# A post-norm transformer layer on one Trainium2 core: attention by chunks of 512 queries and four heads, with fp32r two-part scores and V projected last

## What is computed

```python
Q, K, V = X @ Wq + bq, X @ Wk + bk, X @ Wv + bv        # 2048 x 256, 16 heads of 16
scores = einsum('bhqd,bhkd->bhqk', q, k) / sqrt(16)
out = einsum('bhqk,bhkd->bhqd', softmax(scores), v)
out = out.transpose(0, 3, 2, 1).reshape(b, s, 256)     # (feature, head) by token, as one flat row order
x = layernorm(X + out @ Wo + bo)
gate, up = silu(x @ Wg * s_gate), x @ Wu * s_up        # int8 weights, 1024 wide
x = layernorm(x + (gate * up) @ Wd * s_down)
```

## Time and profile before

| | us |
|---|---|
| three runs | 695.58 (median), 695.06, 698.11 |
| span of the profiled execution | 694.9 |
| PE busy | 668.3 (96%) |
| ACT busy | 580.7 (84%) |
| DVE busy | 153.7 (22%) |
| POOL busy | 38.1 (5%) |
| first exponential starts | 53.86 |
| granted TensorE clock, mean | 0.991 |

### The profile page before, as it was taken

One profiled execution on the slowest core, in us unless ns is written; L12 is line 12 of the kernel. 1 busy time (PEld: TensorE's weight loads), 2 busy tenths in 40 slices (PEclk: granted clock), 3 DMA queues, 4 the chain that ended last, 5 costly groups with the idle time before them and its releaser, 6 DMA issues.

```text
span 694.9 us, 10890 instructions
## 1 busy us (share of the span) xinstructions
PE 668.3 (96%) x4002; PEld 259.4 (37%) x4002; DVE 153.7 (22%) x305; ACT 580.7 (84%) x657; POOL 38.1 (5%) x47
## 2 busy tenths in 40 slices
PE   8979999999999999999999999999999999999994
PEld 7852222222222222222222222222222257788884
DVE  6772000000000000000000000000000047756766
ACT  5748999999999999999999999999999943744442
POOL 3215000000000000000000000003000001000002
PEclk9998999999999999999999999999999999999998
DMA  8066132140404041321404040413000000000001
GB/s 233 19 71 69 13 35 31 17 46 3 46 0 46 0 46 12 34 29 17 45 1 46 0 46 0 46 12 34 0 0 0 0 0 1 1 0 32 0 30 60
DMA packets 15428, 19.50 MB, mean 28 GB/s; under 512 B 5912, under 2 KB 12336, under 8 KB 15408
## 3 DMA queue, kind: packets, MB, share of 16 engines
q1 hardware_dynamic: 14592, 18.97, 20.2%
q10 hardware_dynamic: 816, 0.26, 0.1%
HBM read 4.34 MB, written 2.10 MB: 9 GB/s over the span
## 4 chain that ended last, share of the span: by engine, by line
PE 89%; DVE 5%; issue 4%; ACT 1%; POOL 1%; DMA 1%; POOLq 0%; SPq 0%; DVEq 0%
PE ps L1061 37%; PE ps L1087 36%; PE ps L1184 7%; PE ps L1167 4%; PE ps L966 4%; DMA x_tok<-in_L_attn_X 1%; DVE at L769 1%; DVE stats L785 1%; DVE h L870 1%; PE ps L950 1%; DVE r_tmp L831 1%; ACT sg L549 0%; POOL rstd L431 0%; DVE x_tok L778 0%; PE ps L1155 0%
## 5 line engine op out<-in xcount | busy, mean ns | idle before, releaser
L510 ACT ACTIVATE probs<-ps 128x1024 f32<-128x1024 f32 x512 | 495.2, 1021 | 19.8 <-PE ps L1087 12.5
L1061 PE MATMUL ps<-probs,v_slot 128*32 128x512 f32 x2048 | 272.5, 605 | 4.7 <-issue 4.7
L1087 PE MATMUL ps<-q_stack,k_stack 100*128 100x512 bf16 x1024 | 267.6, 385 | 5.6 <-DVE k_stack L675 5.6
L1087 PEld LDWEIGHTS ps<-q_stack,k_stack 100*128 100x128 bf16 x1024 | 79.7, 98 | 280.8 <-ACT probs L510 213.1
L730 DVE TENSOR_SCALAR attn<-ps 128x512 f32 (+1 forms) x16 | 16.4, 1028 | 488.5 <-PE ps L1061 488.5
L1061 PEld LDWEIGHTS ps<-probs,v_slot 128*32 128x32 f32 x2048 | 40.9, 108 | 114.6 <-ACT probs L510 94.7
L549 ACT ACTIVATE sg<-ps,sgate_c 128x512 f32<-128x512 f32 x32 | 22.1, 690 | 46.7 <-PE ps L1184 46.5
L1167 PE MATMUL ps<-wd,h_hi 128*128 128x256 f32 x128 | 32.2, 285 | 2.3 <-DVE r_tmp L831 2.1
L1167 PE MATMUL ps<-wd,h_lo 128*128 128x256 f32 x128 | 31.9, 283 | 0.0
L870 DVE SCALAR_TENSOR_TENSOR h<-ps,sup_c,sg 128x512 f32<-128x512 f32 x32 | 24.0, 750 | 27.0 <-ACT sg L549 26.2
L1167 PEld LDWEIGHTS ps<-wd,h_hi 128*128 128x128 f32 x128 | 24.3, 190 | 4.9 <-DVE r_tmp L831 3.4
(11 more groups left out here) (100 smaller groups left out, 354.4 us busy)
## 6 DMA issues: line engine op xcount, KB each, us to landing
q_stack<-q_parts SPq DMA_DIRECT2D x16, 192.0 KB
k_stack<-k_parts SPq DMA_DIRECT2D x16, 192.0 KB
q_stack<-q_parts SPq DMA_DIRECT2D x16, 128.0 KB
k_stack<-k_parts SPq DMA_DIRECT2D x16, 128.0 KB
x_tok<-in_L_attn_X SPq DMA_DIRECT2D x3, 512.0 KB, 8.5
out<-out_tmp SPq DMA_DIRECT2D x3, 512.0 KB, 2.9
k_stack<-k_parts SPq DMA_DIRECT2D x16, 64.0 KB
q_stack<-q_parts SPq DMA_DIRECT2D x16, 64.0 KB
```

The costliest lines, as they stand in the source:

```text
L510: nc.scalar.activation(probs[:, (j * TT + kt) % 3, 2 * half:2 * half + 2, :].rearrange("p a b -> p (a b)"), ps[:, 2 * ring:2 * ring + 2, : ...
L1061: last = nc.tensor.matmul(ps[32 * q:32 * q + VW, ACC, :], v_slot[slot][:, kt, :], probs[:, n % 3, q, :], start=(kt == 0), stop=(kt == TT - 1))
L1087: last = nc.tensor.matmul(ps[:, 2 * ring + q % 2, :], k_stack[slot][0:ROWS, kt * P:(kt + 1) * P], q_stack[slot][0:ROWS, q * CW:(q + 1) * C ...
```

## The change

Attention is cut by chunks of 512 queries and quads of four heads: 16 steps (`STEPS`), each with all 2048 keys. A unit is one block of 128 keys for four heads of 512 queries, still two exponentials over 1024 columns. Q and K are kept as two fp32r parts; a head's stack has 51 rows (3 for bound and shift, 48 for three products), and the heads of a pair lie at rows 0 and 64 of the array. A slot (two of them) holds four heads, so that K is filled again for each chunk of queries. V is projected behind all of Q and K, DVE adds its bias straight from PSUM (`save_v`), POOL squares. At a step's end DVE copies bank 6 to `attn_q` (one of two), SP writes it to DRAM in another order (`move_out`, four DMAs) and, once per chunk, reads it back turned (`move_in`, two DMAs); DVE scales it in SBUF (`scale_attn`). The 64 transposes are gone. Loops of attention are written out instead of running in `Fori`. The DMA order on SP is: fill of slot s+2, shifts, at each fourth step move_in, then move_out of step s.

```diff
--- before.py
+++ after.py
-    PRODUCTS = [(3, 0, 0), (2, 1, 0), (1, 2, 0)]
-    SROW = sum(n for n, _, _ in PRODUCTS) * HD
-    MROW = SROW + 1
-    ROWS = MROW + 3
+    NQ = 4
+    QUADS = NH // NQ
+    STEPS = CH * QUADS
+    UPS = TT
+    UW = CW // HD
+    SHIFT_ROWS = 2
+    PROD = 1 + SHIFT_ROWS
+    ROWS = PROD + 3 * HD
+    HALF = 64
+    VW = HD + 1
...
+        k_parts = place("k_parts", [P, KO, 2, S], f32r, at)
...
+        k_slot = [place(f"k_slot{i}", [P, 2, S], f32r, at + 16 * KB * i) for i in range(NSLOT)]
...
+        q_slot = [place(f"q_slot{i}", [P, 2, CW], f32r, at + 4 * KB * i) for i in range(NSLOT)]
...
+        at32 = place("at32", [P, KO, VW, CH, UW], f32, at + 24 * KB)
+        attn_q = [place(f"attn_q{i}", [P, HD, UW], f32, at + 41 * KB + 2 * KB * i) for i in range(2)]
...
+        at_dram = nc.dram_tensor("at_dram", [CH, HD, NH, VW, UW], f32).ap()
...
-        V_AFTER = [(0, 1), (2, 3), (4,), (5, 6, 7)]
-        V_BANK = [4, 5, 4, 5, 4, 5, 4, 2]
+        V_BANK = [4, 5, 2, 3, 4, 5, 7, 6]
         NORM_BANK = [6, 7, 0, 1]
+        LAST_SQUARES = NQK - 4
...
+            def load_q(s, slot, hh, done):
+                h, base, c = NQ * (s % QUADS) + hh, HALF * (hh % 2) + PROD, s // QUADS
+                row, ko = HD * (h % HPB), h // HPB
+                dst, src = q_slot[slot].bitcast(f32), q_parts.bitcast(f32)
+                sp.dma_start(dst[base:base + 2 * HD, hh // 2, :],
+                             src[row:row + HD, ko, 0:1, c * CW:(c + 1) * CW].to_broadcast([HD, 2, CW])
+                sp.dma_start(dst[base + 2 * HD:base + 3 * HD, hh // 2, :],
+                             src[row:row + HD, ko, 1, c * CW:(c + 1) * CW]).then_inc(done, 16)
+            def load_k(s, slot, hh, done, first=0, last=S):
+                h, base = NQ * (s % QUADS) + hh, HALF * (hh % 2) + PROD
+                row, ko = HD * (h % HPB), h // HPB
+                dst, src = k_slot[slot].bitcast(f32), k_parts.bitcast(f32)
+                sp.dma_start(dst[base:base + 2 * HD, hh // 2, first:last],
+                             src[row:row + HD, ko, 0:2, first:last]).then_inc(done, 16)
+                sp.dma_start(dst[base + 2 * HD:base + 3 * HD, hh // 2, first:last],
+                             src[row:row + HD, ko, 0, first:last]).then_inc(done, 16)
+            def load_stack(s, slot, done):
+                for hh in range(NQ):
+                    load_k(s, slot, hh, done)
+                    load_q(s, slot, hh, done)
+            def load_shift(s, slot, done):
+                for hh in range(NQ):
+                    at, row = HALF * (hh % 2) + 1, NQ * s + hh
+                    sp.dma_start(q_slot[slot].bitcast(f32)[at:at + SHIFT_ROWS, hh // 2, :],
+                                 shift.bitcast(f32)[row:row + 1, :, :]).then_inc(done, 16)
+            def move_out(s):
+                c = s // QUADS
+                for hh in range(NQ):
+                    sp.dma_start(at_dram[c, :, NQ * (s % QUADS) + hh, :, :].rearrange("r d u -> d r u"),
+                                 attn_q[s % 2][32 * hh:32 * hh + VW, :, :]).then_inc(at_put[s % 2], 16)
+            def move_in(c):
+                for i in range(2):
+                    sp.wait_ge(at_put[i], 16 * NQ * (QUADS // 2) * (c + 1))
+                for ko in range(KO):
+                    sp.dma_start(at32[:, ko, :, c, :], at_dram[c, HPB * ko:HPB * (ko + 1), :, :, :]
+                                 .rearrange("r h d u -> (r h) d u")).then_inc(at_moved, 16)
+            sp.wait_ge(lo_ready, 1)
+            for hh in range(NQ):
+                load_q(0, 0, hh, stack_loaded[0])
+            sp.wait_ge(lo_ready, NQK - 6)
+            for hh in range(NQ):
+                load_k(0, 0, hh, stack_loaded[0], 0, S - CW)
+            sp.wait_ge(lo_ready, NQK - 2)
+            for hh in range(NQ):
+                load_k(0, 0, hh, stack_loaded[0], S - CW, S)
+            sp.wait_ge(lo_ready, NQK)
+            sp.wait_ge(v_psum, TT // 2)
+            load_stack(1, 1, stack_loaded[1])
...
+            load_shift(1, 1, stack_loaded[1])
+            for s in range(STEPS):
+                if s + NSLOT < STEPS:
+                    sp.wait_ge(scores_ready, 2 * UPS * (s + 1))
+                    load_stack(s + NSLOT, s % NSLOT, stack_loaded[s % NSLOT])
+                    load_shift(s + NSLOT, s % NSLOT, stack_loaded[s % NSLOT])
+                if s >= QUADS and s % QUADS == 0:
+                    move_in(s // QUADS - 1)
+                sp.wait_ge(attn_saved, s + 1)
+                move_out(s)
+            move_in(CH - 1)
...
+            act.wait_ge(v_psum, TT // 2)
+            for g in range(2 * UPS * STEPS):
+                u, p = g // 2, g % 2
+                ring = g % 3
+                act.wait_ge(scores_ready, g + 1)
+                if p == 0 and u >= 3:
+                    act.wait_ge(pv_done, u - 2)
+                nc.scalar.activation(
+                    probs[:, u % 3, 2 * p:2 * p + 2, :].rearrange("p a b -> p (a b)"),
+                    ps[:, 2 * ring:2 * ring + 2, :].rearrange("p a b -> p (a b)"),
+                    ACT.Exp, bias=0.0, scale=SCALE).then_inc(exp_done, 1)
...
+            def save_attn(s):
+                dve.wait_ge(pv_done, UPS * (s + 1))
+                if s >= 2:
+                    dve.wait_ge(at_put[s % 2], 16 * NQ * (s // 2))
+                nc.vector.tensor_copy(attn_q[s % 2][:], ps[:, ACC, :].rearrange("p (u r) -> p r u", r=HD)
+                                      ).then_inc(attn_saved, 1)
+            def scale_attn(c):
+                dve.wait_ge(at_moved, 16 * KO * (c + 1))
+                nc.vector.reciprocal(den[:], at32[:, :, HD, c, :]).then_inc(den_ready, 1)
+                dve.wait_ge(den_ready, c + 1)
+                nc.vector.tensor_tensor(at32[:, :, 0:HD, c, :], at32[:, :, 0:HD, c, :],
+                                        den[:].unsqueeze(2).to_broadcast([P, KO, HD, UW]), ALU.mult
+                                        ).then_inc(attn_scaled, 1)
+            for s in range(STEPS):
+                save_attn(s)
+                if s >= QUADS and s % QUADS == 1:
+                    scale_attn(s // QUADS - 1)
+            scale_attn(CH - 1)
...
+            def scores(g):
+                u, p = g // 2, g % 2
+                s, kt, ring = u // UPS, u % UPS, g % 3
+                slot = s % NSLOT
+                if kt == 0 and p == 0:
+                    pe.wait_ge(stack_loaded[slot], loaded(s))
+                    if s < NSLOT:
+                        pe.wait_ge(bound_ready, 2 * (s + 1))
+                    if s == 1:
+                        pe.wait_ge(late_ones, 2)
+                if g == 0:
+                    pe.wait_ge(norms_ready, 2)
+                elif g < 3:
+                    pe.wait_ge(v_ready, 2 * (g + 1))
+                else:
+                    pe.wait_ge(exp_done, g - 2)
+                for half in range(2):
+                    base = HALF * half
+                    last = nc.tensor.matmul(ps[:, 2 * ring + half, :],
+                                            k_slot[slot][base:base + ROWS, p, kt * P:(kt + 1) * P],
+                                            q_slot[slot][base:base + ROWS, p, :], start=True, stop=True)
+                last.then_inc(scores_ready, 1)
+            def prob_times_v(u):
+                s, kt = u // UPS, u % UPS
+                if u == 0:
+                    pe.wait_ge(v_ones, 1)
+                    pe.wait_ge(v_ready, TT // 2)
+                elif kt == 0:
+                    pe.wait_ge(attn_saved, s)
+                pe.wait_ge(exp_done, 2 * (u + 1))
+                for hh in range(NQ):
+                    last = nc.tensor.matmul(ps[32 * hh:32 * hh + VW, ACC, :],
+                                            v_all[:, kt, NQ * (s % QUADS) + hh, :],
+                                            probs[:, u % 3, hh, :], start=(kt == 0), stop=(kt == TT - 1))
+            UNITS = UPS * STEPS
+            for u in range(UNITS):
+                scores(2 * u)
+                scores(2 * u + 1)
+                if u >= 2:
+                    prob_times_v(u - 2)
+            prob_times_v(UNITS - 2)
+            prob_times_v(UNITS - 1)
...
+            pe.wait_ge(attn_scaled, CH)
```

More of the change, by code:

```diff
@@ L119, in layer_program @@
-        at = region(42 * KB)
-        w_raw = place("w_raw", [P, 3, KO * HID], f32, at)
-        w_hi = place("w_hi", [P, 3, KO, HID], f32r, at + 6 * KB)
-        w_lo = place("w_lo", [P, 3, KO, HID], f32r, at + 12 * KB)
-        rest = place("rest", [P, 4, CW], f32, at + 18 * KB)
-        squares = place("squares", [P, 4, S], bf16, at + 26 * KB)
-        attn = place("attn", [P, S // NH // 4, NH, NH], f32, at)
+        at = place_at[0]
+        v_all = place("v_all", [P, TT, NH, VW], f32)
+        w_raw = place("w_raw", [P, 3, KO * HID], f32, at)
@@ L143, in layer_program @@
-        yt_lo = place("yt_lo", [P, KO, S], f32r, at + 16 * KB)
+        squares = place("squares", [P, 4, S], bf16, at + 32 * KB)
```

(50 more changed lines are left out.)

456 lines of the change are left out of this document (149 added, 307 removed).

## The result

The changed kernel takes 709.15 us (median of four runs, 708.35 to 710.62) against 695.64 for the kernel before on the same chip: the ratio is 1.0193, 95% interval 1.0172 to 1.0214. It is slower by 1.9%. The forecast was 722 us, with 655 to 830 as its range. The profiled execution's span is 707.6 us where the forecast's sum came to 721.5.

What follows compares the result with a forecast made beforehand. SP's in-order DMA chain, 33.0 us a step against 29.4 of compute, was taken to bound attention. Last exponential at 571.4, plus 132.1 as before and 18 more behind attention, gave 721.5 of span, 722 us; range 655 to 830.

Steps and rivals of the forecast that it cites:

- The deciding term: Attention's DMA side: SP's in-order fill, shifts and one-engine writes take 33.0 us a step, more than 29.4 of compute.
- The price of a small packet: In move_out: a 128-byte packet costs 12.9 ns, between 7.9 and 18 ns reads; 14.0 us a step on one engine.
- rival 3: In move_out: small writes are dear, each ns above 12.9 costs 15 us; 830 at 20 ns, about 905 at 25; chance 0.15.
- First exponential: Before attention: with V's projection behind, attention's first exponential starts at 49.2 us, 4.7 us earlier; bounds 47 to 53.
- Start of step 15's fill: In attention: step 2's fill starts at 77.0 us; thirteen rounds of 33.0 plus 15 for move_ins put the last at 521.
- Last exponential: End of attention: last fill done at 541 us, exponentials of step 15 until 571.4, against 562.8 before: +8.6.
- Behind attention: Last exponential to first LN1 sum: 31.8 us instead of 15.5, plus 2 for PE's clock: +18 us.
- One step of slack is eaten at once: Start of attention: the single step by which fills run ahead is used up immediately, then SP's chain sets the pace.
- PE's own time: In attention: a unit takes PE 1.5 us, 0.46 scores side by side plus 1.00 V product, so ACT paces compute.
- (1): In attention: SP's chain hides and ACT sets the pace; 670 us, 657 where packets spread; chance 0.32.
- (2): In attention's scores: the heads don't run side by side, PE's unit stays near 2.0 us, 711 us; chance 0.10.
- The signs: PE under 90% busy, one ACT gap a step of 3 us or more, move_out issues 3 us each, paired score starts.

## Why the prediction was right, and where its sizes were off

**The deciding term held.** The forecast put the end of each step on SP's chain: fill, shifts and four writes on one engine, 33.0 us against 29.4 of compute. Measured: rounds of 31.9 to 32.3 us and compute of 29.33. Its reasons held one by one. The 17-row DMA goes at the rate of one engine (11 GB/s in all while it does), where the rule was taken from the 8-row DMA of the earlier trace rows; the Trainium skill, DMA: Bandwidth & Descriptors, How many engines (k), had stated it, and the write in two parts confirms it. The price of a small packet, interpolated between two reads at 12.9 ns, is 11.4 for this write, 12% less; the fear of dear writes (rival 3) is refuted for this size. A fill was to take 18.8 us; in the change its data go from 140.03 to 159.49 us, 19.5 us. Each move_in was to add 5 us; the three rounds with one in them (38.28, 36.62 and 37.57 us) are 5.5 longer on average.

**The sum term by term.** First exponential: forecast 49.2, measured 46.62, 2.6 less. PE's V products ended at 46.09, near the 47 of the sum, but the branch and waits of 1.5 us that stood behind them cost nothing, since the flag had been written long before. The way to the bound was priced too long as well, 46 us where DVE had written it at 41.76, since the wait of some 4 us ahead of GpSimd's reduction did not come again; it didn't matter behind V. Start of step 15's fill: forecast 521, measured 504.95 (the first fill's was 77.0, measured 74.63). Of these 16 us 2.4 are the head and 13.7 the thirteen rounds. The first of these took 29.55 us, not 33.0, since no write held its first issue. The other twelve, without what a move_in adds, took 32.0: the packet's price made them 1.6 us shorter (1088 x 1.5 ns), fill and waits 0.6 longer. The move_ins took 1.4 us more in all. Last exponential: forecast 571.4, measured 561.17, and here errors cancelled. From the start of step 15's fill to its first exponential at 529.65 it was 24.7 us where the sum had 21.0; and not in the sum was the clock after each gap, so that step 15 took 31.5 us for its exponentials (529.65 to 561.17), not 29.4. These 5.8 us hid part of the 16. Behind attention: forecast +18 us, measured +13.4. Save and writes took 14.7 us from 562.32 to 577.02 where the sum had 17.9 for save, latency, four writes and completion, and move_in took 5.2 instead of 7. Head and chain 10.2 too long, this stretch 4.6, the rest 0.9 too short: together 13.9, the distance from 721.5 to 707.6.

**When the chain takes over.** "One step of slack is eaten at once" was wrong. The slack was used up at 3 us a step, and the first wait came behind the scores of step 5. That moved nothing in the sum, because the end of a chain that is the bound throughout depends on its rounds alone.

**PE's own time.** A unit was to take PE 1.5 us; it takes 1.65. The scores of two pairs are 0.67 us, not 0.46. ACT's 0.92 hides it, as it hid the difference between 1.5 and 1.8 in the forecast. The Trainium skill, TensorE: Matmul & The Clock Gate, Part 3, was right that the groups of rows run at once; the gain for two pairs is 0.67 us against an estimated 0.92 here, and in the trace the two of a pair start 3 to 4 ns apart.

**The rivals.** (1) That the chain hides was nearly the whole of the chance given to faster. It didn't hide, since the packets neither spread nor cost under 9.6 ns. Its price was good: 657 for spread packets, 655.98 measured once they were spread. (2) The heads run side by side. Had they not, 711 would have been too low: even with the write spread it was 734 with 128 rows, and 1164 with 51 rows, where the granted clock was half, which no row of the kernel before showed for a busy PE.

**The signs.** PE's share of 89% and its idle time behind a DMA of a slot came as written. The gaps of ACT did not come as one of 3 us or more in each step: they were 6.1 to 8.1 us at the three steps with a move_in and between 0.2 and 3.0 us at the others. Where a gap is short, the step before it had started at the lower clock and taken some 2 us longer. The four issues of move_out took 9.05 us, 2.3 each and not 3.

## What to carry to other kernels

Count a DMA's rows against the 16 engines before its bytes: 17 rows on one engine turned a gain of 5.8% into a loss of 1.9%, and the wait showed up as idle matmuls behind another, healthy DMA. When a chain on a queue is longer than the compute that should hide it, compute its round and multiply; slack at the start only delays the first sign of it. And keep PE at work through a wait if what comes next on it is on the path: 9.6 us of useless products made the next 48 matmuls 3 us shorter and the kernel 1.8 us.

## What was not expected of the hardware

- The same number of fp32r matmuls of 512 columns, PE busy throughout in each case, ran at a granted clock of 1.00 with two heads of 51 rows side by side, at 0.50 with 51 or 64 rows one after another, and at 1.00 again with 128 rows one after another. The times were 656, 1164, 1169 and 734 us. The Trainium skill, TensorE: Matmul & The Clock Gate, Why this matters for your kernels, says that a single matmul of 32 rows takes the time of one of 128. Here the few rows took 1.8 times as long, through the clock (3.84 against 2.11 us a unit).
- The small writes: 128 bytes from SBUF to DRAM at 11.4 ns each on one engine, 11.5 by the doubled write.
- GpSimd's reduction over partitions started 0.14 us after its input in the change (38.00 to 38.14), where in the kernel before 3.8 us lay between (45.71 to 49.48) with nothing to wait for in the profile. What made the difference stays open.
